# Gated delta rule kernel: the last doubling step of the triangular inverse replaced by a two-step solve, with other changes in the same pass

## The chip, the cores and the metric

The kernel runs on one core of one Trainium2 chip. The metric is the device time of one execution in microseconds; the kernel before has a median of 3140.78 us over three runs (3132.66 to 3145.97).

## What is computed

An attention block with a gated delta rule (16 key heads, 32 value heads, head size 128, sequences of 256 steps, 8 of them) runs beside a feed-forward part that retrieves eight experts of each of eight heads by product keys and mixes their rows. The part that the change touches is the recurrence:

```python
def step(state, inp):
    q_t, k_t, v_t, g_t, b_t = inp
    state = state * jnp.exp(g_t)[..., None, None]
    kv_mem = jnp.einsum('bhkv,bhk->bhv', state, k_t)
    delta = (v_t - kv_mem) * b_t[..., None]
    state = state + jnp.einsum('bhk,bhv->bhkv', k_t, delta)
    o = jnp.einsum('bhkv,bhk->bhv', state, q_t)
    return (state, o)
```

After it the output is multiplied by silu(z), normalised by its root mean square, and projected by w_out. All is float32.

## The kernel before, in words

The recurrence is computed in chunks of 128 steps. Within a chunk the update is a triangular system: with A the strictly lower 128x128 matrix of decayed key products, Y = (I - A)^-1 RHS. The kernel holds A transposed (AT) and needs the inverse's transpose XT.

A pass (64 of them, PASSES) takes one key head of one pair of sequences: eight tasks of 128x128 (2 sequences b, 2 chunks c, 2 value heads r; `task(b, c, r)`). It is pipelined over two passes: the front of pass n+1 (projections by Wkq and Wvz, a four-tap convolution, key products, the mask triangle that makes AT, and the 16x16 diagonal blocks' inverse) runs beside the back of pass n (the solve, state, outputs, gating and output projection), and beside a share of the experts' work: VectorE's expert_dots and expert_mix on rows that GpSimd gathers by indirect DMA.

The inverse: AT goes to a DRAM scratch `whole` in two transfers (line 350), the diagonal blocks come back as `bk` (line 352), VectorE inverts them by elimination (`eliminate`, `lower_products`, `lower_sums`, `lower_scaled`, `lower_block`, lines 1240 to 1282) and makes the transpose xrT (line 1384). Both go out into block diagonals (lines 357, 358) and come back as X16 and XT16, two transfers each (lines 362 to 366). Then TensorE doubles the block size in three levels, 16 to 32 to 64 to 128 (LEVELS):

- `level_E(lv)` (line 550): E = A X for eight tasks, in two groups of four, one PSUM bank each. VectorE (`level`, line 1177, at levels 0 and 2) or ScalarE (`second_level`, level 1) copies the blocks below the diagonal into the buffer Es[lv], whose diagonal is one.
- `level_X(lv, g)`: X E into a bank (line 566, left out at the last level) and its transpose (line 573). ScalarE copies them to X and XT (`take_X`, `take_XT`, line 831).

With the full XT of level 2, `four` (line 581) gives Y of chunk 0 in bank 1; VectorE scales it (`scaled_y`, line 1322); TensorE makes the state S and output O0; K S and Q S (line 670); VectorE makes chunk 1's right-hand side (line 1390); `four` gives Y of chunk 1; its product with MT (O1) ends the pass. ScalarE has scaled Q S into QS (line 904), VectorE adds O1 and QS (`second_outputs`, line 1164) at the start of the next pass and gates the sum with z (`second_gated`).

Each engine has its own instruction list, written out by hand in `one_pass`; the order is that of the text, and engines wait for one another by semaphores, counted per pass in `per`. At the end of ScalarE's list stand silu(2), silu_z(0), squares(0), silu(3), silu_z(1). The next pass's difference products on TensorE (line 526) wait for z, its exponentials on ScalarE (line 845) for those products, its E0 for X16's transfers (`inv_in`) and for the scaled Y of chunk 1.

## Time and profile before

| | |
|---|---|
| median of three runs | 3140.78 us |
| the profiled execution, its own time | 3115.73 us |
| its span | 3113.7 us |
| TensorE busy | 2886.9 us, 93% |
| VectorE busy | 2733.2 us, 88% |
| ScalarE busy | 1871.7 us, 60% |
| GpSimd busy | 2050.0 us, 66% |
| mean granted TensorE clock | 0.976 |

In the rows PE is TensorE's matmul stream, PEld its weight loads, DVE VectorE, ACT ScalarE, POOL GpSimd, SP the queue that issues the DMAs. Each float32 matmul shows as two records (x8 is four products), and the end of a record is modelled, so lengths on TensorE are read from one group's start to the next one's. A bracket at the end of a timeline row is idle time of that engine ahead of the row, with what ended it. The span has a routing stage of some 300 us, then the 64 passes.

### The profile page before, as it was taken

Reading aid. Unit: us, or ns where it says so; the run is one execution under the profiler, and the core shown is the slowest. Engines: PE = TensorE matmul, PEld = TensorE weight load, DVE = VectorE, ACT = ScalarE, POOL = GpSimd, SP = SyncE. Lnnn points to the kernel's source line nnn. Section 1 sums busy time; section 2 is a strip of 40 time slices with the busy share of each in tenths; the row PEclk is TensorE's granted clock in tenths of the full one; section 3 lists DMA queues with packets and bytes.
Section 4 is the critical chain, followed back from the end, with each engine's and each line's share of the span. In section 5 each row is a group of like instructions: output and inputs, shape, how many; then the busy total and the mean of one; then the engine's idle time right before and its main releaser. Section 6 shows DMA issues by size and latency. Waiting matters only on the chain.

```text
span 3113.7 us, 56444 instructions
## 1 busy us (share of the span) xinstructions
PE 2886.9 (93%) x18444; PEld 2386.7 (77%) x18444; DVE 2733.2 (88%) x9037; ACT 1871.7 (60%) x4431; POOL 2050.0 (66%) x2397
## 2 busy tenths in 40 slices
PE   7851899999999999999999999999999999999997
PEld 4431688888888888888888888888888888888886
DVE  4997799999998989989998999899998999988895
ACT  4320566666666666666666666666665666666663
POOL 0003677777776777767777777777777777777764
PEclk9985899999999999999999999999999999999998
DMA  2001555555555555555554555555555555555552
GB/s 63 1 1 45 133 138 134 143 144 138 144 135 135 143 139 138 133 137 143 145 138 128 143 144 144 134 137 143 145 138 133 137 144 145 138 144 131 141 143 81
DMA packets 524419, 394.22 MB, mean 127 GB/s; under 512 B 245984, under 2 KB 449760, under 8 KB 524128
## 3 DMA queue, kind: packets, MB, share of 16 engines
q0 software_dynamic: 65536, 201.39, 24.6%
q1 hardware_dynamic: 458592, 189.23, 23.6%
q8 instruction: 148, 2.42, 0.3%
q14 instruction: 143, 1.17, 0.1%
HBM read 345.41 MB, written 45.09 MB: 125 GB/s over the span
## 4 chain that ended last, share of the span: by engine, by line
PE 46%; DVE 34%; DMA 14%; issue 3%; POOL 1%; ACT 1%; SPq 1%; POOLq 1%; DVEq 0%; ACTq 0%
PE ps L550 12%; DMA X<-whole 7%; PE ps L573 7%; PE ps L516 7%; PE ps L566 7%; DVE mix L1237 6%; DMA whole<-xr 6%; PE ps L533 4%; PE ps L540 3%; DVE xr L1253 3%; DVE MT L1313 3%; DVE outer L1249 2%; DVE qkv L1195 2%; DVE prod L1259 2%; DVE prod L1273 2%
## 5 line engine op out<-in xcount | busy, mean ns | idle before, releaser
L965 POOL DMA_INDIRECT rows<-table,idx_all x1024 | 1106.1, 1080 | 572.5 <-DVEq L1343 294.6
L550 PEld LDWEIGHTS ps<-X,AT 128*128 128x128 f32 x3072 | 365.2, 195 | 84.2 <-DMA X<-whole 83.3
L550 PE MATMUL ps<-X,AT 128*128 128x128 f32 x3072 | 388.2, 280 | 32.3 <-DMA X<-whole 31.2
L573 PE MATMUL ps<-XT,E 128*128 128x128 f32 x3072 | 400.7, 277 | 0.0
L1237 DVE SCALAR_TENSOR_TENSOR mix<-rows,zc,mix 128x256 f32<-128x256 f32 x896 | 376.3, 484 | 2.5 <-ACT zc L828 2.5
L573 PEld LDWEIGHTS ps<-XT,E 128*128 128x128 f32 x3072 | 369.2, 192 | 0.0
L1195 DVE SCALAR_TENSOR_TENSOR qkv<-raw,cwkq,qkv 128x510 f32<-128x510 f32 (+2 forms) x384 | 288.3, 751 | 63.3 <-ACT qkv L807 54.2
L806 ACT ACTIVATE raw<-ps 128x512 f32<-128x512 f32 x256 | 152.8, 597 | 310.9 <-PE ps L516 310.9
L957 POOL TENSOR_SCALAR gm<-cst,gn 128x128 f32<-128x128 f32 x512 | 316.2, 630 | 6.7
L949 POOL TENSOR_SCALAR xg<-xg,rms 128x128 f32<-128x128 f32 x520 | 311.8, 611 | 7.0
L566 PEld LDWEIGHTS ps<-E,XT 128*128 128x128 f32 x2048 | 259.8, 192 | 60.6 <-issue 59.8
L1195 DVE SCALAR_TENSOR_TENSOR qkv<-raw,cwv,qkv 128x510 f32<-128x510 f32 (+2 forms) x384 | 294.1, 780 | 6.8
L953 POOL COPY gn<-gates 128x8 f32<-128x8 f32 x64 | 21.1, 330 | 407.6 <-SPq L326 261.4
L831 ACT ACTIVATE XT<-ps 128x512 f32<-128x512 f32 x384 | 228.1, 594 | 82.6 <-PE ps L573 74.7
L904 ACT ACTIVATE QS<-ps,cols 128x128 f32<-128x128 f32 x256 | 72.9, 368 | 338.1 <-PE ps L670 338.1
L566 PE MATMUL ps<-E,XT 128*128 128x128 f32 x2048 | 271.1, 275 | 0.0
L811 ACT ACTIVATE qkv<-qkv 128x512 f32<-128x512 f32 x256 | 160.8, 628 | 167.7 <-DVE qkv L1195 167.7
L526 PE MATMUL ps<-gm,cst 128*128 128x512 f32 x256 | 140.6, 633 | 123.7 <-POOL gm L957 74.3
L516 PE MATMUL ps<-xnT,Wkq 128*128 128x512 f32 x512 | 250.5, 612 | 0.0
L499 PE MATMUL ps<-wo,yT 128*128 128x256 f32 x1040 | 247.0, 381 | 0.0
L1213 DVE CUSTOM_DVE_ANT_0 rows<-rows,h_all 128x128 f32<-128x128 f32 x1024 | 236.5, 288 | 7.4 <-SPq L326 7.4
L516 PE MATMUL ps<-xnT,Wvz 128*128 128x512 f32 x512 | 242.3, 596 | 0.0
(167 smaller groups left out, 6306.8 us busy)
## 6 DMA issues: line engine op xcount, KB each, us to landing
Wvz<-wvz SPq DMA_DIRECT2D x64, 512.0 KB, 3.3
whole<-AT SPq DMA_DIRECT2D x128, 256.0 KB, 4.0
X<-whole SPq DMA_DIRECT2D x128, 256.0 KB, 4.1
XT<-whole SPq DMA_DIRECT2D x128, 256.0 KB, 5.4
wo<-woh SPq DMA_DIRECT2D x65, 256.0 KB, 3.6
Wkq<-wkq SPq DMA_DIRECT2D x64, 256.0 KB, 2.6
rows<-table,idx_all POOLq DMA_INDIRECT x1024
bk<-whole SPq DMA_DIRECT2D x64, 64.0 KB
```

Of the source, the lines that this page charges most:

```text
L499: done = mm(ps[:, 2 + g, c * D:(c + 1) * D], yT[:, task(g, c, r), :], wo[:, r, :], start=r == 0, stop=r == R - 1)
L516: done = mm(ps[:, bank, :], w[:, k, :], xnT[:, k, bass.ds(pn * N, N)], start=k == 0, stop=k == KD - 1)
L550: done = mm(ps[:, g, (a % 4) * P:(a % 4 + 1) * P], AT_b[:, a, :], src[:, a, :], start=True, stop=True)
L566: done = mm(ps[:, 2 + g, (a % 4) * P:(a % 4 + 1) * P], src[:, a, :], E[:, a, :], start=True, stop=True)
L573: done = mm(ps[:, 4 + g, (a % 4) * P:(a % 4 + 1) * P], E[:, a, :], src[:, a, :], start=True, stop=True)
L831: return A(dst[:, 4 * g:4 * g + 4, :], ps[:, bank, :].rearrange("p (a i) -> p a i", a=4), ACT.Copy)
L949: pool.tensor_scalar(xg[:, a, :], xg[:, a, :], rms[:, a:a + 1], None, ALU.mult).then_inc(sm["y_p"], 1)
L957: pool.tensor_scalar(gm[:, a, :], mask(C_LE), gn[:, a:a + 1], None, ALU.mult).then_inc(sm["gm_p"], 1)
L965: pool.indirect_dma_start(rows[:, m, :], None, table[:, :], bass.IndirectOffsetOnAxis(ap=idx_all[:, f // 4, c:c + 1], axis=0)).then_inc(ga ...
L1195: ins = V.scalar_tensor_tensor(out=o, in0=i, scalar=w, in1=o, op0=ALU.mult, op1=ALU.add)
L1213: st.did(V.tensor_tensor_reduce(out=rows[:, k, 0:P], in0=rows[:, k, 0:P], in1=h2_all[:, n // 4, :], scale=1.0, scalar=0.0, op0=ALU.mult, o ...
L1237: sums[s] = st.did(V.scalar_tensor_tensor(out=mix[:, s, :], in0=rows[:, m, P:ROW], scalar=zc[:, 1, m:m + 1], in1=mix[:, s, :], op0=ALU.mul ...
```

## The change

The third doubling level goes. XT after level 1 is exact within each 64x64 diagonal block, and a chunk is solved in two steps: all rows with that XT (the half solve, right in the top 64 rows), ScalarE copies those rows to `top_y`, TensorE multiplies them by the lower left block of A (`carry`, a product over 64 partitions), VectorE adds that to the right-hand side's lower 64 rows (`lower_rhs`), and the same product with XT gives Y. Level 1's X is no longer made. X16 and XT16 come in one transfer each. QS is added by TensorE: identity times QS opens each accumulation of O1 in PSUM, and VectorE gates from PSUM. Projections, products and copies move to other places of their engines' lists, some to other banks; z's activations come ahead of silu(2) and silu(3) at ScalarE's end of pass, and elimination's finish and chunk 1's right-hand side ahead of the first gating and of the output weights on VectorE. finish_out is cut into halves.

```diff
...
+        top_y = sb("top_y", [HP, 2 * R, P])
...
                 sp.wait_ge(sm["inv_out"], at("inv_out", 16))
-                for g in range(2):
-                    sp.dma_start(X16[:, 4 * g:4 * g + 4, :], matrices(1, g)).then_inc(sm["inv_in"], 16)
+                sp.dma_start(X16[:, :, :], matrices(1)).then_inc(sm["inv_in"], 16)
                 sp.wait_ge(sm["invt_out"], at("invt_out", 16))
-                for g in range(2):
-                    sp.dma_start(XT16[:, 4 * g:4 * g + 4, :], matrices(2, g)).then_inc(sm["invt_in"], 16)
+                sp.dma_start(XT16[:, :, :], matrices(2)).then_inc(sm["invt_in"], 16)
...
-                    if lv < len(LEVELS) - 1:
+                    if lv == 0:
                         for a in range(4 * g, 4 * g + 4):
                             done = mm(ps[:, 2 + g, (a % 4) * P:(a % 4 + 1) * P], src[:, a, :], E[:, a, :], start=True, stop=True)
...
+                def carry(c, bank):
+
+                    pe.wait_ge(sm["top_s"], at("top_s", c + 1))
+                    for b in range(2):
+                        for r in range(R):
+                            o = 2 * b + r
+                            done = mm(ps[:, bank, o * P:(o + 1) * P], AT_b[0:HP, task(b, c, r), :], top_y[:, o, :], start=True, stop=True)
+                    done.then_inc(sm["carry_t"], 1)
...
                     level_X(1, 0)
                     level_X(1, 1)
-                    level_E(2)
+                    if place["u"]:
+                        pe.wait_ge(sm["silu_s"], last("silu_s"))
...
                 if front:
+                    pe.wait_ge(sm["w_vz"], at("w_vz", 32))
                     pe.wait_ge(sm["tap_s"], at("tap_s", 4))
-                    products(1, 7)
+                    projection(2)
+                if back:
+                    pe.wait_ge(sm["xt_s"], at("xt_s", 4))
+                    pe.wait_ge(sm["rv_s"], at("rv_s", 4))
+                    four(1, 0, lambda b, r, a: XT[:, a, :], RV).then_inc(sm["half_t"], 1)
+                if front:
                     pe.wait_ge(sm["at_v"], at("at_v", 8))
-                    squares(1, 6)
-                if back:
-                    level_X(2, 0)
-                    level_X(2, 1)
...
+                    products(1, 6)
+                    squares(1, 3)
+                if back:
+                    carry(0, 2)
+                if front:
                     pe.wait_ge(sm["kq_v"], at("kq_v", 1))
...
+                    projection(3)
+                if back:
+                    pe.wait_ge(sm["low_v"], at("low_v", 1))
+                    four(1, 0, lambda b, r, a: XT[:, a, :], RV).then_inc(sm["y0_t"], 1)
...
                     pe.wait_ge(sm["r1_v"], at("r1_v", 4))
+                    four(0, 1, lambda b, r, a: XT[:, a, :], RV).then_inc(sm["half_t"], 1)
+                    finish_out(1, 0)
+                    carry(1, 1)
+                    finish_out(1, 1)
+                    pe.wait_ge(sm["low_v"], at("low_v", 2))
                     four(0, 1, lambda b, r, a: XT[:, a, :], RV).then_inc(sm["y1_t"], 1)
...
-                    four(4, 1, lambda b, r, a: MT_b[:, a, :], Y).then_inc(sm["o1_t"], 1)
+                    pe.wait_ge(sm["qs_s"], at("qs_s", 4))
+                    for b in range(2):
+                        for r in range(R):
+                            a, o = task(b, 1, r), (2 * b + r) * P
+                            mm(ps[:, 4, o:o + P], ident, QS[:, b, r * P:(r + 1) * P], start=True, stop=False)
+                            done = mm(ps[:, 4, o:o + P], MT_b[:, a, :], Y[:, a, :], start=False, stop=True)
+                    done.then_inc(sm["o1_t"], 1)
...
+                def take_top(c, bank):
+                    act.wait_ge(sm["half_t"], at("half_t", c + 1))
+                    A(top_y[:, :, :], ps[0:HP, bank, :].rearrange("p (a i) -> p a i", a=4), ACT.Copy).then_inc(sm["top_s"], 1)
...
-                if front:
-                    silu(2)
+                    take_top(1, 0)
+                if front:
                     silu_z(0)
                 if back:
                     act.wait_ge(sm["out_t"], at("out_t", 2))
                     act.wait_ge(sm["xg_v"], at("xg_v", 4))
                     squares(0)
                 if front:
+                    silu_z(1)
+                    silu(2)
                     silu(3)
-                    silu_z(1)
...
+                def lower_rhs(c, bank):
+
+                    dve.wait_ge(sm["carry_t"], at("carry_t", c + 1))
+                    v = half_tasks(RV, c)[HP:P]
+                    V.tensor_tensor(v, v, ps[HP:P, bank, :].rearrange("p (b r d) -> p b r d", b=2, r=R), ALU.add).then_inc(sm["low_v"], 1)
```

VectorE's list in the back of a pass reads, after the change: expert_dots(0), scores, second gating, level 0 twice, expert_mix(0, 2), taps 0, expert_mix(2, 4), expert_dots(1), strict_part, mean_square, scores, taps 1, expert_mix(4, 7), causal_part, lower_rhs(0), expert_mix(7, 8) and the sum, scaled_y(0), elimination to lower_sums, chunk 1's right-hand side, the rest of the elimination with xrT, first gating, output_weights, lower_rhs(1), one tap, scaled_y(1), five taps, add_outputs.

## Rows read from the trace of the kernel before

**Rows 1.** The page, busy us, share of the span, instructions

```profile
PE 2886.9 (93%) x18444; PEld 2386.7 (77%) x18444; DVE 2733.2 (88%) x9037; ACT 1871.7 (60%) x4431; POOL 2050.0 (66%) x2397
```

**Rows 2.** The page, the chain that ended last, by engine

```profile
PE 46%; DVE 34%; DMA 14%; issue 3%; POOL 1%; ACT 1%; SPq 1%; POOLq 1%; DVEq 0%; ACTq 0%
```

**Rows 3.** TensorE's timeline, E0: start us, us, what, [idle before, releaser]

```profile
336.31 1.95 PE L550 MATMUL ps<-X,AT 128*128 128x128 f32 x16
...
2370.20 3.49 PE L550 MATMUL ps<-X,AT 128*128 128x128 f32 x16 [2.34 <-DMA X<-whole]
...
3060.87 3.79 PE L550 MATMUL ps<-X,AT 128*128 128x128 f32 x16 [3.01 <-DMA X<-whole]
```

**Rows 4.** TensorE's timeline, one pass from 1506.69

```profile
1506.69 2.05 PE L550 MATMUL ps<-X,AT 128*128 128x128 f32 x16 [0.54 <-DMA X<-whole]
1508.58 1.88 PE L516 MATMUL ps<-xnT,Wkq 128*128 128x512 f32 x4
1510.30 1.05 PE L566 MATMUL ps<-E,XT 128*128 128x128 f32 x8
1511.19 1.06 PE L573 MATMUL ps<-XT,E 128*128 128x128 f32 x8
...
1519.16 1.05 PE L566 MATMUL ps<-E,XT 128*128 128x128 f32 x8
...
1524.52 1.04 PE L628 MATMUL ps<-cst,qkv 128*128 128x128 f32 x8
...
1526.51 0.95 PE L540 MATMUL ps<-ones,sq 128*128 128x1 f32 x8
1527.32 2.03 PE L573 MATMUL ps<-XT,E 128*128 128x128 f32 x16
...
1548.43 1.12 PE L526 MATMUL ps<-gm,cst 128*128 128x512 f32 x2 [0.81 <-ACT z L818]
1549.62 1.60 PE L550 MATMUL ps<-X,AT 128*128 128x128 f32 x12
```

**Rows 5.** VectorE's timeline in the same pass

```profile
1507.89 0.73 DVE L1181 COPY_PREDICATED E<-cst,ps 128x512 f32<-128x512 uint32 x1 [0.26 <-PE ps L550]
...
1511.85 2.32 DVE L1195 SCALAR_TENSOR_TENSOR qkv<-raw,cwkq,qkv 128x510 f32<-128x510 f32 x3 [0.69 <-ACT qkv L807]
...
1524.72 0.43 DVE L1183 COPY E<-ps 64x256 f32<-64x256 f32 x1 [0.45 <-PE ps L550]
...
1526.71 0.69 DVE L1305 TENSOR_TENSOR kq<-ps,cst 128x512 f32<-128x512 f32 x1 [1.36 <-PE ps L533]
...
1528.78 3.25 DVE L1237 SCALAR_TENSOR_TENSOR mix<-rows,zc,mix 128x256 f32<-128x256 f32 x8
...
1532.40 0.75 DVE L1322 TENSOR_TENSOR X<-ps,scol 128x256 f32<-128x256 f32 x2
...
1541.74 2.97 DVE L1195 SCALAR_TENSOR_TENSOR qkv<-raw,cwv,qkv 128x510 f32<-128x510 f32 x4
...
1550.36 0.68 DVE L1164 TENSOR_TENSOR QS<-ps,QS 128x512 f32<-128x512 f32 x1
1550.96 0.72 DVE L1181 COPY_PREDICATED E<-cst,ps 128x512 f32<-128x512 uint32 x1
```

**Rows 6.** A window's busy us by engine, granted clock, DMA share, GB/s

```profile
2371.00:2373.00 2.00, 2.00 (x11) 2.00 (x11) 0.73 (x1) 0.00 (x0) 2.00 (x4) 0.50 0.19 25
```

**Rows 7.** ScalarE's timeline, ahead of DT's exponentials

```profile
1504.99 1.28 ACT L845 ACT_TABLE_LOAD   x1
```

**Rows 8.** SP's timeline in the same pass

```profile
1540.72 0.58 SPq L357 DMA_DIRECT2D whole<-xr  x1
...
1544.75 0.93 SPq L363 DMA_DIRECT2D X<-whole  x2
```

**Rows 9.** The transfers of line 363 (X16), then of 366 (XT16)

```profile
DMA to landing us min/median/max: 3.1/4.1/6.4
...
DMA to landing us min/median/max: 4.8/5.4/6.8
```

More of the change, by code:

```diff
@@ L275, in program @@
         XT = sb("XT", [P, TASKS, P])
-        Es = [sb(f"E{lv}", [P, TASKS, P]) for lv in range(len(LEVELS))]
+        Es = [sb(f"E{lv}", [P, TASKS, P]) for lv in range(2)]
         Y = X
+        top_y = sb("top_y", [HP, 2 * R, P])
         RV = sb("RV", [P, TASKS, P])
@@ L691, in _ @@
             finish_transposes()
-            finish_out(0)
-            finish_out(1)
+            for g in range(2):
+                for c in range(2):
+                    finish_out(g, c)
         @block.scalar
@@ L1400, in one_pass @@
                     for d in (2, 3):
+                        tap(2, d)
+                    for d in (1, 2, 3):
                         tap(3, d)
```

136 lines of the change are left out of this document (56 added, 80 removed).

## The prediction

> **What bounds the kernel now.** I read the page's busy shares first: TensorE 93%, VectorE 88%, the others far below [rows 1]. An average doesn't say which one ends last, so I went to the chain of waits: 46% TensorE, 34% VectorE, 14% DMA [rows 2]. No engine alone is the bound; a loop through three of them is. The starts of a solve's first product (E0, line 550) give its length: 336.31 us and, 63 starts later, 3060.87 [rows 3], so a pass takes 43.25 us, and 2724.6 of the span's 3113.7 us are such passes. I take one quiet pass apart, 1506.69 to 1549.62, 42.93 us. In it TensorE is idle 0.81 us ahead of the second difference product [rows 4] and some 0.3 beside each of the two products that frame it; the rest, 41.4 us, is issue without a gap. VectorE's idle brackets in that pass are 0.26, 0.69, 0.45 and 1.36 us [rows 5], with one small piece 2.9 in all, so its work is 40.0 us. Two engines with 41.4 and 40.0 us of work hand data to each other within 42.9.
>
> The mean is 0.32 above that quiet pass. Where the X16 load lands late, TensorE idles 2.34 us (2370.20), its granted clock then stands at 0.50, that is 1.2 of 2.4 GHz [rows 6], and E0 takes 3.49 us instead of 1.95 [rows 3]. About a dozen of the 63 passes are 44 us or longer.
>
> **The change, TensorE.** A group of four 128x128 products starts 0.89 us after the one ahead (1510.30, 1511.19) [rows 4], so a product is 0.223 us. Gone: the X half of level 1 (8 products), E2 (8), XT2 (8), 24 or 5.36 us. New: two half solves (8), two carries (8), four identity products that add QS, 20 or 4.46 us. No row shows a product over 64 partitions. The nearest from below are eight one-column products, 0.81 us (1526.51 to 1527.32) [rows 4]: even a moving operand 128 times shorter costs 0.1 each, so four carry products lie between 0.4 and 0.89, and I take 0.89, as they stream 128 columns like their neighbours. Work: 41.4 - 0.9 = 40.5 us.
>
> **VectorE.** Gone: the QS sum, 0.60 from its start to the next one's (1550.36, 1550.96), and the two E2 copies, 0.43 each [rows 5]. New: two lower_rhs, the same kind of operation as the QS sum (one operand in PSUM, one in SBUF, 512 long), 0.62 each. The second gating reads PSUM now, as the first does already at the same length. Work: 40.0 - 1.46 + 1.24 = 39.8 us.
>
> **ScalarE.** Four copies of about 0.6 us go, two half-height ones of 0.6 come (the length is 512 either way). It is 60% busy [rows 1]: hidden, except where such a copy is a link of the chain, below. The second gating waits for O1 alone now, and QS for TensorE: both are done before their readers come, so nothing.
>
> **End of pass.** The two z activations move ahead of the last two conv activations. The difference products wait for z, and z waited behind silu(3), which waited for VectorE's last tap: that is the 0.81 us [rows 4], and it goes. Late next is the exponential that makes DT, which now has silu(3), 0.6, and its table load, 1.28 [rows 7], between it and the last tap. By my order it ends 0.3 us after projection 0 could start, and level 0's copy holds TensorE 0.5 longer than that: nothing.
>
> **DMA.** X16 and XT16 come in one 512 KB transfer each. Today X16's halves are issued from 1544.75 [rows 8] and E0 follows at 1549.62, 4.8 us; a half lands after 3.1 to 6.4, XT16's after 4.8 to 6.8 [rows 9]. A single transfer has one issue less and the same bytes: between 3.1 and 6.8; I take 4.8. SP issues two DMAs fewer a pass; GpSimd issues as many gathers as before, at 66% busy.
>
> **The new loop.** TensorE and VectorE are less than 1 us apart, so I lay their order out from level 0's first copy.
> - That copy, after which X0 may start: 0.76. Then TensorE has no gap. X0, E1, KK, squares and projection 1 are 8.86 as now (1510.30 to 1519.16); XT1 1.79; transposes, QK and squares 2.80 (1524.52 to 1527.32); projection 2 1.72 (1508.58 to 1510.30); half solve 0.89; carry 0.89 [rows 4]; and 0.32 to hand over (E0 starts at 1506.69, its first half is out 0.89 later, VectorE starts at 1507.89 [rows 4, 5]). Sum 18.0. VectorE has 17.4 us of work in that stretch and waits 0.5 for the carry.
> - From there VectorE leads. From eight mix steps at 1528.78 to the QS sum at 1550.36 it runs without a gap today, 21.58 us [rows 5]. In the new order six of the mix steps (2.43) stand ahead of the carry, and the output weights (1.21), both lower_rhs (1.24) and the second gating (0.80) are in it: 22.4.
> - In it three waits. Y0: from the carry's arrival TensorE needs 2.61 (projection 3 and Y0, less the 0.32 spent), VectorE has 1.78 of work: 0.8. Second carry: from Y0's arrival TensorE needs 0.80 for the scaled Y, then S, O0, two half outputs, KS, QS, projection 4, half solve, ScalarE's copy of 0.6 and the carry, 10.8; VectorE has 9.34 (1532.40 to 1541.74) [rows 5] and 1.21: 0.25. Y1: 1.94 against lower_rhs and one tap, 1.36: 0.6. Together 1.7. Queued behind the first of them on VectorE are the last mix steps, their sum (which frees the rows buffer for GpSimd's gathers) and the whole elimination, and so the next pass's X16; behind the last, the taps and the output sums.
> - Loop: 18.0 + 22.4 + 1.7 = 42.1 us, 1.15 under 43.25. TensorE then idles 1.6 us in five or six pieces, none near 2 us, so I expect no fall of its clock.
> - X16's load: the inverse ends 32.7 us after E0, the load is issued 4.0 later as now (1540.72, 1544.75) [rows 8] and lands at 41.5, just ahead of E0; another 0.5 late costs nothing, as level 0's copy is the later wait.
> - Another queue that moves: the block load bk is issued some 19.9 us after E0 and elimination starts at 24.8, earlier by 1.6 than now (it stands right behind 1532.40). That leaves 4.9 us for a load of 64 KB, where X16's halves of 256 KB land after 4.1 in the middle and 6.4 at most [rows 9]. Mostly hidden; if it slips, elimination waits.
>
> 63 passes at 1.15 are 72 us. The passes ahead of the loop and behind it I take at zero, within 3: there the longer chain (half solve, copy, carry, sum, 3.5 us a chunk) stands against 5.4 us of products. The profiled execution, 3115.73 us with a span of 3113.7, would be 3043; it lies 25 us under the median of 3140.78. Work doesn't vary from run to run, waits do, and late loads are what the new order absorbs, so I carry half of the 25. **3055 us.**
>
> A rule speaks against the carry: the Trainium skill, TensorEngine Tiling, section Tiling Modes, says that a change of the array's tiling mode drains TensorE. If a product over 64 partitions is such a change, a pass has four. It gives no price, and no run so far shows one.
>
> **Rivals.**
> 1. TensorE stays the bound and only its net four products count: 0.89 x 63 = 56 us, 3085. For it: 93% busy. Against: it also loses the 0.81 us wait.
> 2. TensorE stalls going into and out of each carry. From zero (groups of different shapes follow each other without a bracket in rows 4) to 0.5 a change (the 0.32 hand-over plus the 0.17 by which a group's record, 1.06, outlasts its 0.89). There are four a pass, and in my order 3.5 of them lengthen the loop. Nearest are the gapless neighbours, so the forecast has zero; 0.1 to 0.25 makes 42.4 to 43.0, 3070 to 3110.
> 3. Slower: the same place at its upper end. At 0.33 a change the gain is gone (1.15 / 3.5), at 0.5 the loop is 43.85, 38 us more than before, and with the same half of the 25 the time is 3166. For it speaks only that no row shows such a product.
> 4. The loads collide: VectorE's release of the rows buffer comes later after E0, so the last gathers run under X16's load. If that lands 1.4 us later than today in each pass, half a us is lost: 3087. Parity wants 2 us in every pass, beyond today's slowest half.
> 5. The change does only its end of pass: the 0.81 us goes and turns up at once in the wait for X16, since that load hangs on elimination: 3140. This holds if the solve doesn't bring elimination forward; by my order it ends 32.7 us after E0 instead of 34.0.
>
> **Numbers.** Forecast 0.55; rivals 1, 2 and 4 (3070 to 3120) together 0.30; faster than 3012 0.03; rival 5 0.07; rival 3 0.05. A measurement of this kernel can tell 0.5% (16 us) from no change: faster 0.88, same 0.07, slower 0.05. The range goes from 3012 (half a us less of waiting in each pass, 41.6, and none of the 25 carried) to 3108, rival 2's upper end.
>
> **What would show it.** Difference products and E0 without a bracket, or under 0.3; TensorE's granted clock at 1.00 from 400 us on; carries of 0.89 from start to start, with nothing behind them; VectorE idle 0.5 and 0.25 before lower_rhs, 0.8 and 0.6 before the scaling of Y; passes of 42.1. A bracket at the work behind a carry says rival 2 or 3; one at E0 says 4; one ahead of the first elimination step says that bk was late.

## The result, and the profile after

Forecast were 3055 us and a range of 3012 to 3108. Measured were 3164.05 us (3147.95 to 3190.69, 4 runs) beside 3136.72 us for the kernel before (3126.03 to 3145.97, 4 runs): 1.0102 of the time before, 95% interval 1.0058 to 1.0146. The changed kernel is slower by 1.0%, and the prediction is wrong in its direction and its range. The experiments below found that this figure has two parts, one of the kernel and one that depends on the chip or the session: the same code took 3090.07 us (0.9873, 0.9846 to 0.9899) and 3084.53 us (0.9821, 0.9806 to 0.9836) on chip B, and 3153.11 us (1.0027, 0.9999 to 1.0054) on chip C. Four chips, called A to D here, served the experiments; the first measurement's isn't known. One execution of all those below, in experiment 14, took 10436.86 us and is left out of its ratio.

The page of the changed kernel, first measurement: busy shares, chain by engine, two groups (their last columns are busy us, mean ns, then idle us ahead of them and what ended it), and two transfers with the us to landing.

```profile
PE 2898.9 (92%) x17932; PEld 2333.3 (74%) x17932; DVE 2718.3 (86%) x8972; ACT 1791.8 (57%) x4303; POOL 2036.9 (65%) x2396
...
PE 69%; DVE 14%; ACT 7%; issue 5%; DMA 3%; POOL 1%; POOLq 1%; SPq 0%; another core or an unknown queue 0%; DVEq 0%; ACTq 0%
...
L1250 DVE SCALAR_TENSOR_TENSOR mix<-rows,zc,mix 128x256 f32<-128x256 f32 x896 | 394.1, 496 | 76.1 <-ACT zc L855 74.1
...
L580 PE MATMUL ps<-RV,XT 128*128 128x128 f32 x2048 | 276.8, 278 | 43.9 <-ACT RV L904 37.2
...
whole<-AT SPq DMA_DIRECT2D x128, 256.0 KB
X<-whole SPq DMA_DIRECT2D x64, 512.0 KB, 4.7
```

TensorE has 512 matmul records fewer than in [rows 1] (256 products, four a pass), yet is busy 12 us longer. DMA has fallen from 14% of the chain to 3% [rows 2]. New is ScalarE, 7%: VectorE waits 74.1 us for its expert scores (zc) and TensorE 37.2 us for RV, 1.16 and 0.58 us a pass, in places where the forecast has no wait. The transfer of AT has lost its landing time; it comes back below.

TensorE's timeline of one pass, the changed kernel, first measurement:

```profile
1511.61 1.95 PE L549 MATMUL ps<-X,AT 128*128 128x128 f32 x16
1514.06 1.95 PE L515 MATMUL ps<-xnT,Wkq 128*128 128x512 f32 x4 [0.51 <-ACT DT L872]
...
1526.89 1.04 PE L637 MATMUL ps<-cst,qkv 128*128 128x128 f32 x8
...
1530.40 1.13 PE L580 MATMUL ps<-RV,XT 128*128 128x128 f32 x8 [0.54 <-ACT RV L904]
...
1532.26 0.95 PE L539 MATMUL ps<-ones,sq 128*128 128x1 f32 x8
1533.14 1.16 PE L589 MATMUL ps<-top_y,AT 64*128 64x128 f32 x8
1534.23 1.98 PE L515 MATMUL ps<-xnT,Wvz 128*128 128x512 f32 x4
1536.05 1.05 PE L580 MATMUL ps<-RV,XT 128*128 128x128 f32 x8
...
1545.97 1.03 PE L497 MATMUL ps<-wo,yT 128*128 128x256 f32 x4
1546.93 1.16 PE L589 MATMUL ps<-top_y,AT 64*128 64x128 f32 x8
1548.02 1.13 PE L497 MATMUL ps<-wo,yT 128*128 128x256 f32 x4
1548.99 1.05 PE L580 MATMUL ps<-RV,XT 128*128 128x128 f32 x8
...
1555.11 1.05 PE L549 MATMUL ps<-X,AT 128*128 128x128 f32 x8
```

The pass is 43.50 us, against 42.1 forecast. Two things stand out. The carries (L589, "64*128 64x128") have no bracket but take 1.09 us from start to start instead of 0.89, and what stands beside them is stretched as well: the projection behind the first carry takes 1.82 us to the next group instead of 1.72 [rows 4], the half output ahead of the second 0.96 instead of 0.86 (its spacing in the 128-row version of experiment 2). And the half solve waits for RV.

ScalarE's timeline of the same pass says why RV is late:

```profile
1526.68 0.60 ACT L858 ACTIVATE XT<-ps 128x512 f32<-128x512 f32 x1 [0.20 <-PE ps L572]
1528.20 0.60 ACT L858 ACTIVATE XT<-ps 128x512 f32<-128x512 f32 x1 [0.93 <-PE ps L572]
1528.70 1.56 ACT L904 ACTIVATE RV<-ps,norm 128x256 f32<-128x256 f32 x4
1530.12 0.23 ACT L855 ACTIVATE zc<-zc 128x8 f32<-128x8 f32 x1
...
1552.52 0.60 ACT L841 ACTIVATE z<-ps 128x512 f32<-128x512 f32 x1 [2.06 <-PE ps L519]
```

The transposes (L637) start at 1526.89, so the XT products ahead of them were all issued by then, but ScalarE takes the second group only at 1528.20, after standing idle for 0.93 us. z's product group, 1549.88 and 1.89 long in the full timeline, is taken at 1552.52, 0.75 us after its end. In the semaphore events of this trace, TensorE's increment for the second XT group comes at 1528.18, 1.13 us after the record of its last product ends; the median over the passes is the same.

### The profile page after: what moved, and what is told of

It is laid out like the page before. It is cut to its first block, busy times and chain, and to the rows that moved or that the text cites. A ratio compares the mean times of both kernels' runs of the same rounds, so it can differ in the third digit from the quotient of the medians.

```text
span 3146.1 us, 55163 instructions
## 1 busy us (share of the span) xinstructions
PE 2898.9 (92%) x17932; PEld 2333.3 (74%) x17932; DVE 2718.3 (86%) x8972; ACT 1791.8 (57%) x4303; POOL 2036.9 (65%) x2396
## 3 DMA queue, kind: packets, MB, share of 16 engines
q14 instruction: 142, 1.16, 0.1%
## 4 chain that ended last, share of the span: by engine, by line
PE 69%; DVE 14%; ACT 7%; issue 5%; DMA 3%; POOL 1%; POOLq 1%; SPq 0%; another core or an unknown queue 0%; DVEq 0%; ACTq 0%
PE ps L515 11%; PE ps L580 10%; PE ps L572 9%; PE ps L497 6%; PE ps L519 5%; PE ps L549 4%; PE ps L565 4%; PE ps L589 4%; PE ps L532 3%; ACT RV L904 3%; PE ps L677 3%; PE ps L539 3%; DVE qkv L1208 3%; ACT L872 2%; PE ps L525 2%
## 5 line engine op out<-in xcount | busy, mean ns | idle before, releaser
L1250 DVE SCALAR_TENSOR_TENSOR mix<-rows,zc,mix 128x256 f32<-128x256 f32 x896 | 394.1, 496 | 76.1 <-ACT zc L855 74.1
L580 PEld LDWEIGHTS ps<-RV,XT 128*128 128x128 f32 x2048 | 259.8, 192 | 138.0 <-issue 118.9
L580 PE MATMUL ps<-RV,XT 128*128 128x128 f32 x2048 | 276.8, 278 | 43.9 <-ACT RV L904 37.2
L515 PE MATMUL ps<-xnT,Wkq 128*128 128x512 f32 x512 | 252.0, 615 | 22.5 <-ACT DT L872 22.4
L572 PEld LDWEIGHTS ps<-XT,E 128*128 128x128 f32 x2048 | 249.8, 192 | 30.1 <-issue 29.9
L549 PEld LDWEIGHTS ps<-X,AT 128*128 128x128 f32 x2048 | 243.4, 192 | 38.0 <-issue 20.4
L572 PE MATMUL ps<-XT,E 128*128 128x128 f32 x2048 | 260.8, 276 | 0.0
L1226 DVE CUSTOM_DVE_ANT_0 rows<-rows,h_all 128x128 f32<-128x128 f32 x1024 | 243.7, 300 | 19.1 <-DVE mix L1250 12.2
L549 PE MATMUL ps<-X,AT 128*128 128x128 f32 x2048 | 251.2, 276 | 3.3 <-DMA X<-whole 2.9
L519 PE MATMUL ps<-Wvz,xnT 128*128 128x256 f32 x1024 | 243.2, 381 | 0.0
L804 ACT ACTIVATE yT<-xg 128x128 f32<-128x128 f32 x516 | 152.9, 297 | 136.7 <-issue 108.5
L810 ACT ACTIVATE yT<-ps,nwc 128x512 f32<-128x512 f32 x130 | 82.4, 683 | 226.1 <-PE ps L489 202.2
L519 PEld LDWEIGHTS ps<-Wvz,xnT 128*128 128x128 f32 x1024 | 190.8, 191 | 24.0 <-issue 0.5
```

The source lines that it names most:

```text
L515: done = mm(ps[:, bank, :], w[:, k, :], xnT[:, k, bass.ds(pn * N, N)], start=k == 0, stop=k == KD - 1)
L519: done = mm(ps[:, bank, (t % 2) * 256:(t % 2) * 256 + 256], xnT[:, k, pn * N + t * P:pn * N + (t + 1) * P], Wvz[:, k, 2 * P:4 * P], start= ...
L549: done = mm(ps[:, g, (a % 4) * P:(a % 4 + 1) * P], AT_b[:, a, :], src[:, a, :], start=True, stop=True)
L572: done = mm(ps[:, 4 + g, (a % 4) * P:(a % 4 + 1) * P], E[:, a, :], src[:, a, :], start=True, stop=True)
L580: done = mm(ps[:, bank, o:o + P], lhs(b, r, a), rhs[:, a, :], start=True, stop=True)
L1226: st.did(V.tensor_tensor_reduce(out=rows[:, k, 0:P], in0=rows[:, k, 0:P], in1=h2_all[:, n // 4, :], scale=1.0, scalar=0.0, op0=ALU.mult, o ...
```

## The experiments

Each is an edit of the changed kernel unless it says "before". The kernel before was run on the same chip with each, and ratios are to it.

**1. The scores ahead of the second XT copy** (chip A).

```
-                    for g in range(2):
-                        take_XT(1, g)
+                    take_XT(1, 0)
+                    silu_scores(1)
+                    take_XT(1, 1)
...
-                    silu_scores(1)
```

> The changed kernel with ScalarE's second expert scores placed between its two copies of the second XT, where it stood idle 0.9 us, instead of behind the eight RV scalings. Theory A (ScalarE's queue order makes the loss: VectorE's second expert sum waits 1.11 us for the scores, 74 us in 64 passes): that wait falls under 10 us in all, and the pass (median 43.5 us now) shortens by 0.2 to 0.8 us, as VectorE's first half is behind the lower right-hand sides. Theory B (TensorE and its carry set the first half; VectorE's wait there is only slack in front of its 0.64 us wait for the carry): the wait moves to the carry and the kernel stays within 0.3% of the changed one.

3067.66 us, 0.9815 (0.979 to 0.9841). Far more than theory A allowed, and more than the edit can do: ScalarE's second XT copy, which it doesn't speed up, was on time. That pointed away from the order of the queue and to the execution itself. What the edit does by itself is seen beside the unedited kernel without late increments (experiment 5, on another chip): a pass of 42.47 us against 42.73, 22 us in the whole, with TensorE's waits for ScalarE's exponentials (DT) at 6.5 us in all instead of 22.4. By which way the earlier scores shorten that wait wasn't traced.

**2. Carries over all 128 rows** (chip A).

```
-        top_y = sb("top_y", [HP, 2 * R, P])
+        top_y = sb("top_y", [P, 2 * R, P])
...
-    done = mm(ps[:, bank, o * P:(o + 1) * P], AT_b[0:HP, task(b, c, r), :], top_y[:, o, :], start=True, stop=True)
+    done = mm(ps[:, bank, o * P:(o + 1) * P], AT_b[:, task(b, c, r), :], top_y[:, o, :], start=True, stop=True)
...
+            pool.memset(top_y[:, :, :], 0.0).then_inc(zeroed, 1)
```

> The changed kernel with the carry products over all 128 rows: top_y keeps 128 partitions with its lower half zero, and the weights are all rows of AT, so TensorE's tile size never changes; the result is the same. Theory B (each carry over 64 rows costs TensorE 0.2 us of its own and 0.1 us in the group on either side, some 0.35 to 0.4 us, because the array is emptied at the change of tile size): start to start of the carry falls from 1.09 to 0.89 us, the group ahead of it by 0.1 us, the pass by 0.5 to 0.8 us, the kernel by 35 to 50 us. Theory A (the extra is a wait that the profile hides, for ScalarE's copy of the upper half): the same 1.09 us stays and nothing is gained.

3044.63 us, 0.9742 (0.9714 to 0.9771). TensorE's timeline, 128-row carries:

```profile
1281.70 0.95 PE L539 MATMUL ps<-ones,sq 128*128 128x1 f32 x8
1282.51 1.14 PE L589 MATMUL ps<-top_y,AT 128*128 128x128 f32 x8
1283.48 1.88 PE L515 MATMUL ps<-xnT,Wvz 128*128 128x512 f32 x4
...
1295.13 1.03 PE L497 MATMUL ps<-wo,yT 128*128 128x256 f32 x4
1295.99 1.14 PE L589 MATMUL ps<-top_y,AT 128*128 128x128 f32 x8
1296.96 1.03 PE L497 MATMUL ps<-wo,yT 128*128 128x256 f32 x4
```

The squares ahead are back to 0.81 us, the half output to 0.86, the carry itself is 0.97 (not 0.89: 0.08 remains; the state product and the pass's first product with X, which start behind a wait, take 0.96 and 0.97 as well, but no wait is recorded ahead of the carry, so what the 0.08 is stays open). Its pass is 42.07 us in the median, 42.10 in the mean: the 42.1 of the forecast, which had priced the change of shape at nothing. Set against the unedited kernel without late increments (experiment 5, chip B), the pass is 0.66 us shorter and the kernel 45 us faster, as theory B said. Two chips are compared there; experiment 6, beside experiment 5 on chip B, finds the same with the scores moved as well.

**3. The transposes ahead of the second XT products** (chip A).

```
-                    level_X(1, 0)
-                    level_X(1, 1)
                     if place["u"]:
                         pe.wait_ge(sm["silu_s"], last("silu_s"))
                     for t in range(4):
...
                             done.then_inc(sm["v_t"], 1)
+                    level_X(1, 0)
+                    level_X(1, 1)
```

> The changed kernel with the eight V transposes ahead of the second step's XT products on TensorE instead of behind them (ScalarE's order unchanged). In the changed kernel ScalarE's copy of the second XT group starts 1.1 us after the records end its products, and the transposes' semaphore increments come with it in a burst. Theory C (the transposes behind the products hold back the products' increments): the copy starts within 0.3 us of the end of its products, RV is done 1 us earlier, the wait of 0.54 us for RV is gone and the pass is 0.3 to 0.6 us shorter. Theory D (whatever holds the increments back lies in the time, with the DMA traffic, not in the order): the second XT copy, or what stands in its place, is still about 1 us late.

3122.27 us, 0.9991 (0.9967 to 1.0015). This chip shows no late increments, so the run can't choose between C and D. What it shows instead is the price of the order: with the second XT copy, and RV behind it, 0.7 us later on ScalarE (16.19 and 16.69 us into the pass, against 15.49 and 15.99 in experiment 5), VectorE waits 57.5 us in all for the scores and TensorE 21.0 us for RV. The pass is 43.34 us, 0.6 longer than the unedited kernel's.

**4. Split loads** (chip A).

```
-     sp.dma_start(X16[:, :, :], matrices(1)).then_inc(sm["inv_in"], 16)
+     for g in range(2):
+         sp.dma_start(X16[:, 4 * g:4 * g + 4, :], matrices(1, g)).then_inc(sm["inv_in"], 16)
```

> The changed kernel with each of the two 512 KB loads of the inverses split in two again, as in the kernel before. If the single loads help as forecast (X lands 4.7 us after issue instead of 6.4 us for the second half), splitting makes the wait of the first product for X larger and the pass 0.2 to 0.6 us longer. If the landing hides under the other waits at the seam (ScalarE's exponentials), it stays within 0.3%. If the single load is what holds back TensorE's increment at the end of the pass (ScalarE's z copy 1.4 us late), the copy comes on time at 40.1 us instead of 41.5 us, and the pass is up to 0.6 us shorter.

3091.39 us, 0.9886 (0.986 to 0.9912), against 3090.07 unedited (0.9873, on chip B): no difference, and the median pass is 42.73 us in both. TensorE waits 28.9 us for X instead of 5.5, but 6.7 instead of 22.4 for ScalarE's exponentials behind it: the second outcome, a landing that hides under the next wait at the seam.

**5. The changed kernel again** (chip B), and **9.** a third time (chip B).

> The changed kernel, not edited. Three small edits each gave far more than they could (ScalarE's scores moved: 3067.7 us; split loads: 3091.4 us), and in none of the four profiles are TensorE's semaphore increments late, which they were in the changed kernel's. Theory E (the late increments were a condition of the chip or the session in which the changed kernel was timed): it now takes 3065 to 3100 us, 1 to 2% less than the kernel before, with ScalarE's second XT copy at about 15.1 us after the pass begins. Theory F (they belong to this very order of instructions, and any of the edits breaks them): 3145 to 3190 us again, with the copy at 16.5 us.

> The changed kernel, not edited, timed a third time, beside the kernel before on the same chip. So far 3164.05 us (1.0102 of the kernel before) in one session and 3090.07 us (0.9873) in another. If the slow outcome belongs to a chip or session and is rare: 3083 to 3095 us again and a pass of 42.7 us. If it comes with each session by chance: 3148 to 3190 us, a pass of 43.5 us, and ScalarE's copy of the second XT group 16.5 us after the pass begins.

3090.07 us (0.9873, 0.9846 to 0.9899) and 3084.53 us (0.9821, 0.9806 to 0.9836): theory E. ScalarE's timeline in a pass of the fifth run that begins at 1366.26 and ends at 1408.99:

```profile
1381.03 1.32 ACT L858 ACTIVATE XT<-ps 128x512 f32<-128x512 f32 x2
1382.25 1.57 ACT L904 ACTIVATE RV<-ps,norm 128x256 f32<-128x256 f32 x4
1383.69 0.22 ACT L855 ACTIVATE zc<-zc 128x8 f32<-128x8 f32 x1
...
1405.69 0.60 ACT L841 ACTIVATE z<-ps 128x512 f32<-128x512 f32 x1 [1.34 <-PE ps L519]
```

Both XT copies run back to back; RV begins 15.99 us after the pass begins instead of 17.09. TensorE's timeline of the same pass:

```profile
1384.36 1.05 PE L580 MATMUL ps<-RV,XT 128*128 128x128 f32 x8
...
1386.15 0.95 PE L539 MATMUL ps<-ones,sq 128*128 128x1 f32 x8
1387.03 1.16 PE L589 MATMUL ps<-top_y,AT 64*128 64x128 f32 x8
1388.11 1.98 PE L515 MATMUL ps<-xnT,Wvz 128*128 128x512 f32 x4
1389.93 1.05 PE L580 MATMUL ps<-RV,XT 128*128 128x128 f32 x8
```

The wait for RV is gone, the half solve starts 18.10 us into the pass instead of 18.79, and from there to the next pass it is 24.63 us against 24.71. So of the 0.77 us between the two passes 0.69 lies ahead of the half solve. The carries cost here what they cost there. VectorE's whole wait for the scores is 3.0 us, against 74.1.

**6. 128-row carries and the scores moved** (chip B), and **17.** again (chip D).

> The changed kernel with both the 128-row carry products and ScalarE's scores placed between its copies of the second XT. If the first run's gain came from the scores (3067.7 us) and the second's from the carry (3044.6 us), together they give 3030 to 3040 us; if the scores' place is worth nothing once TensorE's increments are on time (VectorE waits 0.84 us for the carry anyway), it stays at 3040 to 3048 us.

> The changed kernel with 128-row carries and ScalarE's scores between the XT copies, timed again, for a second chip. On a chip without late increments it took 3043.49 us (0.9734). There again: 3038 to 3052 us. On one with them: with the scores ahead of the late copy, VectorE's expert sum no longer waits for it, and the carries are 0.7 us a pass cheaper, so 3060 to 3110 us, still 1 to 2.5% under the kernel before.

3043.49 us (0.9734, 0.9707 to 0.9761) and 3042.45 us (0.9682, 0.9656 to 0.9708). The scores' place, 0.26 us a pass beside 64-row carries (experiment 1), is worth nothing beside full ones (42.06 us against 42.07 in experiment 2): VectorE then waits for the carry instead. This is the fastest version found, 2.7 to 3.2% under the kernel before; chip D had no late increments either, so how it does with them wasn't seen.

**7. QS summed by VectorE again** (chip B), and **12.** the same with 128-row carries.

```
+                        dve.wait_ge(sm["qs_s"], last("qs_s"))
-                    gated(1, ps[:, 4, :], rq2[nx], z2[nx])
+                    second_outputs()
...
-                            mm(ps[:, 4, o:o + P], ident, QS[:, b, r * P:(r + 1) * P], start=True, stop=False)
-                            done = mm(ps[:, 4, o:o + P], MT_b[:, a, :], Y[:, a, :], start=False, stop=True)
+                    four(4, 1, lambda b, r, a: MT_b[:, a, :], Y).then_inc(sm["o1_t"], 1)
```

> The changed kernel with QS joined by VectorE's sum again, in its old place ahead of the first level's mask copies, with the gating behind the first expert sum, and only four products for the second output on TensorE. Forecast of the working: TensorE's seam is 0.9 us shorter, VectorE 0.65 to 0.7 us longer; since VectorE bounds most of the pass from the elimination on but TensorE bounds the seam up to the next pass, the pass is 0.3 to 0.7 us shorter if TensorE's end (identity products before the differences) sets the pass, and 0.2 to 0.7 us longer if VectorE does.

> The changed kernel with 128-row carries and with QS joined by VectorE's sum as in the kernel before. With full carries TensorE has only 0.5 us of idle time in a pass of 42.07 us and VectorE some 2.4 us. Theory (TensorE is now the bound): without the four identity products, 0.89 us of TensorE's work, for 0.65 us more of VectorE's, the pass is 0.1 to 0.5 us shorter, 3012 to 3037 us. Rival (the loop through both is the bound, so that work moved from one to the other changes nothing, as with 64-row carries, 3087.4 against 3090.1 us): 3037 to 3047 us.

3087.41 us (0.9862, 0.9827 to 0.9896) against 3090.07: nothing either way. TensorE comes to the seam 0.9 us sooner and waits there, 41.1 us for the exponentials and 17.8 us for X in all (22.4 and 5.5 unedited). With full carries 3057.29 us (0.9739, 0.9725 to 0.9753): above both expectations. Its counterpart is experiment 2, which differs in QS alone: by the ratio the two can't be told apart (0.9742), by the pass of the profiled executions the twelfth is 0.3 us longer (42.36 against 42.07), so the theory falls and the rival holds or is exceeded. Less work for TensorE gains nothing: it waits 46.9 us for X instead of 10.4, and 19.1 for the exponentials instead of 7.1. Where QS is joined gains nothing here. The "0.5 us of idle time" of the expectation counts the brackets alone. Read from start to start, which is how the forecast counts, TensorE's groups in experiment 2 take about 1.5 us more than their usual spacings: 0.31 ahead of projection 0, 0.48 ahead of the first product with X, 0.22 ahead of the state product, the rest in six pieces of 0.07 to 0.10.

**8. Before, with the new end of the pass alone** (chip B).

```
-                    silu(2)
                     silu_z(0)
...
-                    silu(3)
                     silu_z(1)
+                    silu(2)
+                    silu(3)
```

> The kernel before with the new end of the pass alone: ScalarE takes z0, the squares and z1 first and both last SiLUs behind them, and TensorE waits for them ahead of the V transposes of the next pass. The differences come one after the other at about 40.3 us instead of at 40.3 and 42.0 us, with ScalarE's exponentials behind them. Theory (TensorE waits at the seam for ScalarE's z1, so this part is worth something by itself): 20 to 60 us faster than before. Rival (the loads of X and XT end the seam anyway, at 42 to 43 us, so that nothing is gained): within 0.5% of before.

3129.58 us, 0.9998 (0.9975 to 1.0021): the rival. TensorE's waits (us in total, times, longest) in this run:

```profile
PE ps L550 <- DMA X<-whole: 92.1, 63, 3.9
```

and in the kernel before, unedited (experiment 16):

```profile
PE ps L550 <- DMA X<-whole: 44.1, 42, 4.1
PE ps L526 <- ACT z L818: 35.6, 62, 0.8
```

The wait for z, 35.6 us, is gone, and the wait for X has taken it over, 44.1 to 92.1. (In the first profile of the kernel before they are 37.8 and 31.2: the wait for X differs by 13 us between two executions of the same kernel, the step to 92.1 is far beyond that.) That is what the forecast's rival 5 says of this part.

**10. Carry products and half outputs in turn** (chip B). Eight changes of the tile size at the second carry instead of two, same products.

```
-                    finish_out(1, 0)
-                    carry(1, 1)
-                    finish_out(1, 1)
+                    for k in range(4):
+                        a, c, r = task(k // R, 1, k % R), k // R, k % R
+                        done = mm(ps[:, 1, k * P:(k + 1) * P], AT_b[0:HP, a, :], top_y[:, k, :], start=True, stop=True)
...
+                        done = mm(ps[:, 3, c * D:(c + 1) * D], yT[:, task(1, c, r), :], wo[:, r, :], start=r == 0, stop=r == R - 1)
```

> The changed kernel with the four products of the second carry and the four half-output products behind it issued in turn (64 rows, 128 rows, 64, 128 ...) instead of four and four. Same products, but eight changes of the tile size there instead of two. Theory (each change costs, because the weights of the next product are not loaded under the product before: about 0.09 us in and 0.2 us out, and 0.09 in the group ahead; some 0.37 us for a pair of changes): these eight products take 1.1 us longer from first to last, and the carry is out 0.9 us later, so the pass grows by 0.5 to 1.1 us, 3120 to 3160 us. Rival (the extra belongs to the 64-row product itself, not to the change): nothing changes, 3090 us.

3247.68 us, 1.034 (1.0323 to 1.0357). TensorE's timeline at that place:

```profile
1277.96 0.46 PE L690 MATMUL ps<-top_y,AT 64*128 64x128 f32 x2 [0.77 <-ACT top_y L851]
1278.35 0.70 PE L693 MATMUL ps<-wo,yT 128*128 128x256 f32 x2
1278.98 0.48 PE L690 MATMUL ps<-top_y,AT 64*128 64x128 f32 x2
...
1280.02 0.48 PE L690 MATMUL ps<-top_y,AT 64*128 64x128 f32 x2
...
1282.34 1.16 PE L580 MATMUL ps<-RV,XT 128*128 128x128 f32 x8 [0.15 <-DVE RV L1340]
```

A carry product and a half-output product, 0.22 and 0.43 us where the size stays, take 1.04 together (1278.98 to 1280.02). So two changes cost 0.39 us, **one change 0.195**, in and out alike (0.19 and 0.20). The expectation had the right price and too small a sum: 45.02 us a pass, 2.3 more. The three further pairs are 1.17 of it; 0.77 is the wait for ScalarE's copy, which the first half output had covered and now doesn't. The rest, 0.35, I put to the half outputs, which now stand ahead of the last carry product; no run shows it.

The weight loads of the fifth run, around the carry of its pass, show where the 0.195 goes:

```profile
1387.03 0.96 PEld L589 LDWEIGHTS ps<-top_y,AT 64*128 64x128 f32 x8
1388.11 0.30 PEld L515 LDWEIGHTS ps<-xnT,Wvz 128*128 128x128 f32 x2
```

and behind the 128-row carry of experiment 2:

```profile
1283.37 0.30 PEld L515 LDWEIGHTS ps<-xnT,Wvz 128*128 128x128 f32 x2
```

The first load of each size starts at the same time as its first product (1387.03, 1388.11); with one size the projection's first load starts 0.11 us ahead of its product (1283.37, 1283.48), under the last product of the carry. So that much of the load isn't hidden at a change. Projection 3's first product also holds the second back by 0.1 us longer than in the 128-row version.

**11. ScalarE's old end of pass** (chip B).

```
+                    silu(2)
                     silu_z(0)
...
+                    silu(3)
                     silu_z(1)
-                    silu(2)
-                    silu(3)
```

> The changed kernel with ScalarE's old order at the end of the pass: SiLU 2, z0, squares, SiLU 3, z1. Theory (in the new order VectorE's taps come last, so z0 and z1 behind the SiLUs hold the differences, the exponentials and the first product): z1 comes at about 43 us instead of 39.4 us after the pass begins, the second difference product waits over 1 us, and the pass is 1 to 2.5 us longer, 3150 to 3250 us. Rival (X's landing ends the seam as well): under 0.3 us a pass, below 3110 us.

3128.6 us, 0.9958 (0.9941 to 0.9974), 44 us over the 3084.53 measured beside it. The mechanism is the one named, its size, 0.57 us a pass, about half of the least that was expected and beyond the rival's 0.3: z1 at 41.7 us (medians), a pass of 43.30 us against 42.73.

```profile
1248.09 1.10 PE L525 MATMUL ps<-gm,cst 128*128 128x512 f32 x2
1250.38 1.12 PE L525 MATMUL ps<-gm,cst 128*128 128x512 f32 x2 [1.19 <-ACT z L841]
```

The second difference product waits 1.19 us, but the two waits behind it at the seam (0.51 and 0.15 in the unedited kernel) go in exchange. So the new end of pass is worth nothing on the kernel before and 0.57 us a pass on the two-step solve, which has moved VectorE's taps to the end.

**13. The changed kernel, fourth time** (chip C).

> The changed kernel, not edited, timed a fourth time. Two sessions gave a pass of 42.73 us (3090.07 and 3084.53 us); the first one gave 43.5 us and 3164.05 us, with TensorE's increments late at two places. Either 3080 to 3095 us with all copies on time, or 3145 to 3190 us with ScalarE's second XT copy at 16.5 us and its z1 at 41.5 us; a time in between would say that something else differed.

3153.11 us, 1.0027 (0.9999 to 1.0054). The pass is 43.47 us in the median, ScalarE's second XT copy stands at 16.52 us into it behind 0.92 us of idle time, and TensorE waits 36.4 us for RV: the first measurement once more, on a known chip.

**14. ScalarE held back on purpose** (chip C).

```
+                def hold(k0, k1):
+                    for k in range(k0, k1):
+                        act.wait_ge(sm["hold_s"], at("hold_s", k))
+                        A(spare[:, :], mask(C_LE, 4), ACT.Copy).then_inc(sm["hold_s"], 1)
...
                     act.wait_ge(sm["xt_t"], at("xt_t", 2 * lv + g + 1))
+                    if lv and g and front:
+                        hold(0, 2)
...
                     act.wait_ge(sm["proj_t"], at("proj_t", 5 + n))
+                    if n and back:
+                        hold(2, 5)
```

> The changed kernel with ScalarE held back on purpose at the two places where TensorE's increments reached it late in the changed kernel's profile: two copies of 512 numbers between the arrival of the second XT group and its copy (1.1 us, so that it starts at about 16.5 instead of 15.4 us), three of them between the arrival of projection 5's second half and the z1 copy (1.5 us, 41 us instead of 39.4 us). No product is moved. Theory (the late arrival at these two places is what lies between 3090 and 3164 us): the pass grows from 42.73 to 43.3 to 43.7 us and the kernel takes 3125 to 3160 us. Rival (the lateness was only in the records, and the time went elsewhere): the kernel stays under 3105 us.

3309.19 us, 1.0497 (1.0457 to 1.0538). The run fell on the chip with late increments, so the delay came on top of theirs, and the numbers expected don't apply. ScalarE's timeline:

```profile
1468.70 1.30 ACT L870 ACTIVATE spare<-cst 128x512 f32<-128x512 f32 x2 [0.92 <-PE ps L573]
1469.90 0.58 ACT L861 ACTIVATE XT<-ps 128x512 f32<-128x512 f32 x1
...
1493.67 1.96 ACT L870 ACTIVATE spare<-cst 128x512 f32<-128x512 f32 x3 [1.52 <-PE ps L520]
1495.53 0.58 ACT L844 ACTIVATE z<-ps 128x512 f32<-128x512 f32 x1
```

Added were 1.20 us at the first place and 1.86 at the second; the pass grew from 43.47 to 46.14 us (medians), the half solve came 1.47 later (18.72 to 20.19 us into the pass, 0.45 of it ahead of projection 0, which waits longer for the exponentials). ScalarE, "60% busy" [rows 1], has no slack left at these two places: a delay there costs most of itself. It refutes "only in the records" in so far as a wait at this copy reaches the pass. It doesn't by itself measure the first 1.1 us; the comparison of experiments 5 and 13 does.

**15. Before, with single loads alone** (chip C).

```
-    for g in range(2):
-        sp.dma_start(X16[:, 4 * g:4 * g + 4, :], matrices(1, g)).then_inc(sm["inv_in"], 16)
+    sp.dma_start(X16[:, :, :], matrices(1)).then_inc(sm["inv_in"], 16)
```

> The kernel before with the single 512 KB loads of X16 and XT16 alone. The forecast priced them at nothing beyond fewer late landings (one issue less, the same bytes); splitting them in the changed kernel changed nothing (3091.39 against 3090.07 us). If the loads matter where the pass is bound by X16's arrival, as the kernel before is in its passes of 44 us and more: 10 to 30 us faster than before. If only the bytes count: within 0.3%.

3107.81 us, 0.9884 (0.9859 to 0.9909), 35 us by the medians: of the two parts tried on the kernel before, the one that gains by itself.

```profile
PE ps L524 <- ACT z L816: 37.7, 62, 0.8
PE ps L548 <- DMA X<-whole: 23.0, 39, 2.9
```

The wait for X is 23.0 us, against 31.2 and 44.1 in the two profiles of the kernel before, and 3 of the 63 passes are 44 us or longer, against 14 and 25. Those two were taken on other chips; their executions took 3115.73 and 3132.62 us, this one 3105.81, so the kept profiles show 10 to 27 of the 35 us. The profile of this run has TensorE's increments late as well, at its XT products 14 us into the pass (0.74 us in the median), and still it gains.

**16. The kernel before again** (chip D, for its profile).

> The kernel before, not edited, for its profile on the chip at hand. On the chip of the fourth timing the changed kernel's profile has TensorE's increments late again (3153.11 us; the kernel before 3143.09 us there), on two others it has not. If the lateness is the chip's and meets every kernel, the kernel before has late copies there too (its second X and XT copies, behind the products at 13 to 16 us of the pass) and loses less by them; on a chip without it, every copy follows its products by 0.2 us.

3132.62 us. Chip D shows no lateness, so whether the unedited kernel before has it on chip C wasn't seen; its profile there wasn't taken. It ran at 3143.09 us on chip C and at 3125.16 to 3139.57 us on the others. Experiment 15 makes it likely that it has, at a small cost.

## Why the prediction was wrong

- **The carry**, "I take 0.89", with "zero" for the change of shape: the term that failed in the kernel itself. Measured is 0.195 us a change where 64 and 128 rows alternate (experiment 10), and 0.66 us a pass between experiments 5 and 2, which is 0.165 for each of its four changes. The mechanism was written down, as rival 2 (0.1 to 0.25 a change, 3070 to 3110 us; by its own 3.5 changes the lower end is 3077), and with 0.195 and the forecast's 3.5 changes in the loop it gives 42.1 + 0.68 = 42.8 us; measured are 42.73 (experiments 5 and 9), 3090 and 3084.5 us. The "gapless neighbours" of [rows 4] were all of one size on the array, so they bore on nothing; they should not have set the value, nor 0.89 stand as the upper end. The rule weighed there, in the Trainium skill's TensorEngine Tiling (Array Packing), section Tiling Modes, is that a change of mode drains TensorE. The trace agrees in so far as it shows a loss at the change: 0.97 us for the same carry over 128 rows, 1.08 over 64, and a weight load that isn't pulled ahead on either side.
- **ScalarE** "hidden, except where such a copy is a link of the chain": the second step that failed, and the larger. Its work was priced, the moment at which it hears of its input wasn't. On chip C, and in the first measurement, TensorE's increments reach it some 1.1 us late behind the second XT products. The half solve then stands 0.69 us later, and the pass is 0.73 to 0.77 us longer: 46 to 49 us in 63 passes, the larger part of the 63 to 80 us between the measurements. The rest is in passes of 44 us and more, none in experiments 5 and 9, 13 in the first measurement (mean 43.71, median 43.50) and 9 in the thirteenth; they lose their time mostly ahead of the second Y1 product and of O1, and why wasn't traced. Neither profile of the unedited kernel before shows such lateness. No rival had it; that rival 3's 3166 us came within 2 us of the measured time is luck, for it stands on 0.5 us a change.
- **The sum**: the profiled execution took 3147.95 us, 105 over the 3043. The passes of experiment 5 (mean 42.69) against 42.1 are 37 of that, with the carry as their cause; those of the first measurement (43.71) against experiment 5 are 64, some 49 of them the late increments in the median pass and the rest the long passes; 4 lie outside the loop. "Half of the 25", the allowance between the profiled execution and the median, was 16 us in the first measurement and nothing in experiment 5 (3089.88 and 3090.07), whose time lies inside the stated range although its carry term failed.
- **Right**: the loop. Without the change of size the pass is 42.07 us, and the profiled execution of experiment 2 took 3046.20 us against "3043". TensorE's 40.5 us hold there (42.07 less some 1.5 of idle time, read from start to start; 1.6 were forecast), and the waits of VectorE came near: in experiment 5 it waits 0.92 and 0.43 us ahead of the two lower_rhs (forecast 0.5 and 0.25), 0.67 and 0.48 ahead of the scaling of Y (0.8 and 0.6). The granted clock falls in 1 of the 63 passes of experiment 5, in 7 in the profile of the kernel before. bk was in time, as there is no bracket ahead of elimination.

```profile
1388.22 0.69 DVE L1334 TENSOR_TENSOR RV<-RV,ps 64x512 f32<-64x512 f32 x1 [0.92 <-PE ps L589]
...
1402.01 0.69 DVE L1334 TENSOR_TENSOR RV<-RV,ps 64x512 f32<-64x512 f32 x1 [0.43 <-PE ps L589]
```

- **End of pass**: "it goes", 0.81 us, and it went; alone it is worth nothing (experiment 8), together with the new order of VectorE 0.57 us a pass.
- **DMA**: X lands after 4.7 us (4.8 forecast) in one transfer. That the single load has a worth of its own on the kernel before, 1.2%, was missed: its halves land at up to 6.4 us [rows 9], and with one transfer the long passes are nearly gone. In the changed kernel that worth is zero, for the late landing hides under the exponentials (experiment 4).
- **Identity join**: priced at 0.9 us of TensorE against 0.60 of VectorE; on the changed kernel it moves nothing (experiment 7).
- **The granted clock** explains neither: its mean over the execution is 0.977 in the first measurement and 0.974 in experiment 5, whose span is 58 us shorter.

What stays open: what holds the increments back on chip C and in the first measurement. In the four profiled executions that show it (the first measurement, 13, 14, 15) the page has no landing time for the transfers of AT (L351), in all others it has, 3.5 to 4.0 us; their traces hold 32900 to 34500 semaphore events, those of the others 44600 and more. Gaps in the records and lateness come together, so the recording itself may hold the increments back, or something else holds back both. A time taken without a recording would tell; that wasn't tried. Of four measurements of the unedited changed kernel two show it.

## What to carry to other kernels

Half the rows on TensorE are not cheaper rows: a product over 64 partitions among products over 128 costs 0.195 us at each change, and padding the operand with zeros to 128 partitions, at the same streaming time, gave the 42.07 us that a forecast without the cost has (3044.6 against 3090 us). Before a wait is optimized away at a seam, look which wait is next there: the end of pass on the kernel before and the loads in the changed kernel each moved a wait and changed nothing. And if three small, unlike edits all gain more than they can, run the unedited kernel again, on another chip, before explaining them.

## What was not expected of the hardware

- The same code differs by up to 2.6% between measurements (3084.5 and 3164.05 us) while the kernel before differs by 0.6% (3125.16 to 3143.09 us). In the slow ones TensorE's increments come 1.1 us behind the products' records. That the kernel before has slack where they come late is likely from experiment 15, not shown. Whether it goes by chip or by session is known for chip B alone, where two sessions agree.
- The size of the tile costs on the neighbours: the group ahead of a carry is 0.07 to 0.10 us longer, the projection behind the first one 0.10.
- TensorE with 0.5 us in brackets, and some 1.5 us of idle time from start to start, in a pass of 42.07 us was not the bound: 0.89 us of its work given to VectorE made the pass no shorter (0.3 us longer in the profiled execution).
